# A decoder layer on one core: feed-forward weight pieces rounded and cast by ScalarE, limited by GpSimd, and the attention stage's side work put at other steps

## The chip, the cores and the metric

The kernel runs on one core of a Trainium2 chip. The metric is the device time of one execution in microseconds; each kernel is given with the median of its runs. The profile is of one execution of its own.

## The reference

One decoder layer over x (4 x 512 tokens x 512) and a context (4 x 512 x 256), in three stages that each end in a layer norm:

```python
x = _layernorm(x + _L0_attn_ref(x, q, k, v, o weights and biases))   # 32 heads of 16
x = _layernorm(x + _L0_xattn_ref(x, ctx_1024, Wq, bq, Wk, bk))
x = _layernorm(x + _L0_ffn_ref(x, w_gate, w_up, w_down))             # 512 -> 2048 -> 512
```

The attention quantizes its weights to 4 bits, and its activations in chunks of 64 tokens: per chunk the channel bias is taken away, each channel gets one of 8 scales by comparing its maximum with thresholds, and values are rounded to that scale. The same is done again to the attention's result before the output projection. The feed-forward weights are ternary:

```python
scale = jnp.clip(jnp.mean(jnp.abs(w)), EPS)
q = jnp.clip(jnp.round(w / scale), -1.0, 1.0) * scale
```

## The kernel before, in words

Everything is written out by hand for the five engines; each engine runs its own list in order and waits on semaphores. There are three stages: preparation (sums of weights, x decomposed), the attention stage, and the rest (output projection, cross attention, feed-forward). The change is in the attention stage.

**Groups and steps.** The attention stage goes through 32 groups (`NG`), numbered n = 0 to 31: batch b = n // 8, four heads r = n % 8. Each group has 8 steps, u = 0 to 7, and every engine has a function for one group: `pe_period`, `act_period`, `dve_period`, `pool_period`, `sp_period`. "Even" groups are those with n even. In the text a time "in the group" is counted from the group's transpose of the row maxima (`pe_nm`, L1134), which TensorE issues at the end of step 1. A group's length is the time from its transpose to the next one.

**TensorE** does in each step twice: a 128x512 score tile of the next group (`pe_scores`, L1129, three banks, so tile t waits until VectorE has read tile t - 3), and a transposed score tile of an earlier group (`pe_scores_T`, L1150, three banks, so tile t waits until ScalarE has taken the exponential of tile t - 3). At four steps, `PV_AT`, it multiplies a quarter of the probabilities by the values (`pe_pv`, L1164). In even groups it projects the next tile of queries and keys at steps 3 and 5 (`QK_AT`, `pe_qk`, L333 and L334), in odd groups the values at step 5 (`pe_v`, L1115 and L1117).

**VectorE** takes a maximum of each score tile (`dve_max`, L1277), splits the 16 maxima of a group in three bf16 terms at steps 0 and 1 (`dve_nm`, L1284 to L1293) for the transpose, scales queries and keys (`dve_y`, L353), and does the side work in `dve_context`, after the tiles of the step: for the attention's result of batch b - 2 the maximum (`dve_tmax`), eleven threshold steps (`dve_levels`), and the final values (`dve_n`, L1017).

**ScalarE** takes the exponentials (L1237, two per step), copies pieces out, and at step 3 of groups 0 to 23 rounds one piece of the feed-forward weights by adding a large constant (`act_ffn`, L1393, 128x1024 f32 in place). `act_round` (L1013) rounds the attention's result at r = 3.

**GpSimd** works the query and key parts (`pool_parts`), normalizes (`pool_norm`), and finishes a weight piece in two operations (`pool_ffn`): L1399 limits it to the constant plus or minus 1, L1401 takes the constant away and writes bf16 into `f_int_all`. Then it centers (`pool_center`, r = 7) or scales (`pool_scale`, r = 1) the attention's result.

**SyncE** issues the DMAs in one order: the transposed maxima, stacks of queries and keys, in odd groups the spread of the reciprocal sums and the attention's result (`sp_spread`, which for b >= 2 waits until all of `dve_n` of two batches before is done), stores, and the next weight piece (`sp_ffn`). The ring for weight pieces has two slots.

```python
PV_AT, QK_AT, V_AT, HIGH_AT, MIDDLE_AT = (1, 2, 6, 7), (3, 5), 5, (4, 6), (5, 7)
```

Of the kernel before, what the change touches and what calls it, by code (L numbers as in the profile page):

```python
# [18 lines left out]
P = 128  # L19
# [28 lines left out]
def decoder_layer(nc, io):  # L48
    whole = ExitStack()
    with whole:  # L50
# [19 lines left out]
        had = keep("had", [P, P])  # L70
        magic = keep("magic", [P, 1])
        chunk_of = keep("chunk_of", [96, NB, S], BF16)
        n_T = keep("n_T", [P, KD, NB, S], BF16)
# [329 lines left out]
        with stage:  # L403
# [194 lines left out]
            with nc.Block() as block:  # L598
# [135 lines left out]
                @block.gpsimd  # L734
                def _(pool):
                    pool.memset(onesf[:], 1.0)
                    pool.memset(sv_col[:], 1.0)
# [330 lines left out]
        with stage:  # L1068
# [37 lines left out]

            PV_AT, QK_AT, V_AT, HIGH_AT, MIDDLE_AT = (1, 2, 6, 7), (3, 5), 5, (4, 6), (5, 7)
            def v_bank(kt):
# [143 lines left out]
            def act_period(act, g):  # L1252
                even = g.h == 0
                for u in range(8):
# [5 lines left out]
                    if even and g.has(2):  # L1260
                        if u in HIGH_AT:
                            act_high(act, g.tile(2), HIGH_AT.index(u))
                        if u in MIDDLE_AT:
                            act_middle(act, g.tile(2), MIDDLE_AT.index(u))
                    if g.b > 1 and g.r == 3 and 1 <= u <= 4:
                        act_round(act, g.b - 2, u - 1)
                    if u == 3 and g.n < PIECES:
                        act_ffn(act, g.n)
                    if not even and u == V_AT + 1 and g.b < NB - 1:

                        if g.b and g.s == 0:
                            act.wait_ge(pv_mm, 2 * 2 * KD * g.b)
                        act_v(act, g.b + 1, g.s)
# [39 lines left out]
            def dve_context(dve, g, u):  # L1313
# [10 lines left out]
                if g.b > 1 and g.r == 0:  # L1324
                    if u == 0:
                        dve_tmax(dve, g.b - 2, misc)
                    else:
                        dve_levels(dve, g.b - 2, u - 1)
                if g.b > 1 and g.r == 1 and u < 4:
                    dve_levels(dve, g.b - 2, 7 + u)  # L1330
                if g.b > 1 and g.r == 3 and u > 4:
                    dve_n(dve, g.b - 2, u - 5)
                if g.b > 1 and g.r == 4 and u == 0:
                    dve_n(dve, g.b - 2, 3)
                if g.b == NB - 1:
# [8 lines left out]
            def pool_period(pool, g):  # L1344
                if g.h == 0 and g.has(2):
                    pool_parts(pool, g.tile(2))
                if g.h == 1 and g.n >= 5:
                    pool_norm(pool, (g.n - 5) // 2, rs_bc[:])
                if g.n < PIECES:
                    pool_ffn(pool, g.n)  # L1350
                if g.b and g.r == 7:
                    for ct in range(KD):
                        pool_center(pool, g.b - 1, ct)
                if g.b > 1 and g.r == 1:
                    for ct in range(KD):
                        pool_scale(pool, g.b - 2, ct)

            def sp_pv(sp, g):
# [4 lines left out]
            def sp_period(sp, g):  # L1363
# [16 lines left out]
                if g.n == PIECES:  # L1380
                    need(sp, "f_done", 2 * PIECES)
                    load_wo(sp, woT[:], bo_row[:])
# [4 lines left out]
            def sp_ffn(sp, c):  # L1387
                need(sp, "f_done", 2 * (c - 1))
                sp.dma_start(f_ring[:, c % 2, :], io["ffn"][c]).then_inc(f_in[c % 2], 16)
# [6 lines left out]
            def pool_ffn(pool, c):  # L1396
                raw = f_ring[:, c % 2, :]
                need(pool, "f_round", c + 1)
                did(pool.tensor_scalar(raw, raw, MAGIC - 1.0, MAGIC + 1.0, ALU.max, ALU.min), "f_done")  # L1399
                need(pool, "f_done", 2 * c + 1)  # L1400
                did(pool.tensor_scalar(f_int_all[:, c, :], raw, -MAGIC, None, ALU.add), "f_done")  # L1401

# [923 lines left out]
```

## Time and profile before

| what | before |
|---|---|
| median of 3 runs | 1176.83 us (1174.73 to 1180.32) |
| time of the profiled execution | 1178.66 us |
| its span | 1176.9 us |
| PE busy | 955.5 us (81%) |
| DVE busy | 863.0 us (73%) |
| ACT busy | 688.4 us (58%) |
| POOL busy | 388.9 us (33%) |

The busy shares are averages over three stages. The attention stage lies from about 142 us to 619 us of the span.

### The profile page before, as it was taken

To read this page: it belongs to the slowest core of one execution; us is meant where nothing else is said; L and a number is where in the kernel's file an instruction comes from. 1 tells how busy PE (TensorE), PEld (TensorE's weight loads), DVE (VectorE), ACT (ScalarE), POOL (GpSimd) and SP (SyncE) were. 2 spreads that over 40 slices of the span, in tenths; PEclk is the share of its full clock that TensorE was granted. 3 is DMA by queue.
4 is the path that set the end of the run, shared out by engine and by line. 5 is a ranking of instruction groups with operands and counts; after the bars stand their busy time and mean duration, and the time that the engine had idled before them with its cause. 6 is when DMAs were issued, how large, how long until landed. Compare 5 with 4: busy or idle time off the path is not lost. (4 is left out here: it accounts for less than half of the span.)

```text
span 1176.9 us, 13444 instructions
## 1 busy us (share of the span) xinstructions
PE 955.5 (81%) x4128; PEld 369.3 (31%) x4128; DVE 863.0 (73%) x1622; ACT 688.4 (58%) x1103; POOL 388.9 (33%) x303
## 2 busy tenths in 40 slices
PE   3667799889998888988887678797989798879465
PEld 1223322222222222222122343343434343434122
DVE  7996688888899989999883658568656765575245
ACT  3778377777777677767564034265526562555255
POOL 4103355656665676653002423130014001400000
PEclk9779699999999999999999879999999899989788
DMA  8966455555556554546334102310251025002500
GB/s 306 350 234 213 163 153 164 170 180 181 182 181 181 163 172 153 177 138 178 92 101 137 56 38 64 80 72 1 58 120 73 1 53 120 7 1 61 118 1 36
DMA packets 90684, 145.00 MB, mean 123 GB/s; under 512 B 12339, under 2 KB 52147, under 8 KB 89078
## 3 DMA queue, kind: packets, MB, share of 16 engines
q1 hardware_dynamic: 90614, 144.16, 40.7%
q8 instruction: 33, 0.54, 0.2%
q14 instruction: 37, 0.30, 0.1%
HBM read 84.75 MB, written 42.21 MB: 108 GB/s over the span
## 5 line engine op out<-in xcount | busy, mean ns | idle before, releaser
L1277 DVE TENSOR_REDUCE neg_max<-banks 128x1 f32<-128x512 f32 x512 | 331.4, 683 | 48.2 <-PE banks L1129 44.7
L1237 ACT ACTIVATE probs<-banks 128x512 f32<-128x512 f32 x512 | 278.3, 600 | 116.3 <-PE banks L1150 115.5
L1129 PE MATMUL banks<-k_st,q_st 96*128 96x512 bf16 x512 | 198.0, 392 | 20.9 <-DVE neg_max L1277 18.4
L1150 PE MATMUL banks<-q_st,k_st 99*128 99x512 bf16 x512 | 195.4, 385 | 13.2 <-ACT probs L1237 9.3
L1164 PE MATMUL banks<-probs,v_st 128*32 128x512 f32 x1024 | 137.1, 607 | 17.5 <-ACT pv_z L1250 16.3
L1543 POOL TENSOR_TENSOR rstd<-vare,half 128x1 f32<-128x1 f32 x48 | 26.8, 558 | 358.7 <-DVE vare L1535 358.7
L1749 PE MATMUL banks<-q_T,f_int_all 128*128 128x512 bf16 x512 | 127.5, 391 | 19.5 <-DVE h_ring L1770 19.4
L1129 PEld LDWEIGHTS banks<-k_st,q_st 96*128 96x128 bf16 x512 | 50.4, 99 | 171.2 <-DVE neg_max L1277 105.3
L1808 PE MATMUL banks<-hz,I_h 128*128 128x512 f32 x128 | 67.9, 667 | 34.5 <-DMA hz<-h_turned 32.1
L1759 DVE TENSOR_TENSOR h_ring<-banks,gate_row 128x512 f32<-128x512 f32 x64 | 44.1, 689 | 60.3 <-PE banks L1749 58.5
L1399 POOL TENSOR_SCALAR woT<-woT 128x1024 f32<-128x1024 f32 x24 | 87.2, 3633 | 2.4 <-ACT woT L1393 0.4
L1764 ACT ACTIVATE h_ring<-h_ring 128x512 f32<-128x512 f32 x64 | 40.3, 630 | 79.5 <-DVE h_ring L1759 79.5
L1749 PEld LDWEIGHTS banks<-q_T,f_int_all 128*128 128x128 bf16 x512 | 49.0, 100 | 101.2 <-DVE h_ring L1770 28.8
L1787 ACT COPY h_turned<-banks 128x512 f32<-128x512 f32 x64 | 37.1, 582 | 61.1 <-DMA hz<-h_turned 36.3
L1150 PEld LDWEIGHTS banks<-q_st,k_st 99*128 99x128 bf16 x512 | 49.9, 98 | 64.7 <-ACT probs L1237 22.1
L1891 PE MATMUL banks<-f_int_all,ctx_q 128*128 128x512 bf16 x256 | 61.1, 386 | 9.1 <-ACT ctx_q L1875 9.1
L1527 PE MATMUL banks<-attn_T,x_T 128*128 128x512 f32 x128 | 60.8, 619 | 9.1 <-DVE x L1566 7.5
L906 POOL TENSOR_TENSOR ctx_q<-ctx_q,rs_bc 128x512 f32<-128x512 f32 x14 | 17.8, 1269 | 151.7 <-DMA ctx_q<-pv_rows 151.7
L1827 DVE TENSOR_TENSOR h_max<-h_abs,h_max 128x512 f32<-128x512 f32 x60 | 45.0, 751 | 30.7 <-ACT h_abs L1816 29.4
L1401 POOL TENSOR_SCALAR f_int_all<-woT 128x1024 bf16<-128x1024 f32 x24 | 66.7, 2778 | 2.0
L1813 ACT COPY hz<-banks 128x1024 f32<-128x1024 f32 x32 | 32.4, 1014 | 58.8 <-PE banks L1808 58.7
L1781 PE MATMUL banks<-h_ring,had 128*128 128x512 f32 x128 | 64.4, 596 | 2.1 <-ACT h_turned L1787 2.1
(263 smaller groups left out, 1519.1 us busy)
## 6 DMA issues: line engine op xcount, KB each, us to landing
hz<-h_turned SPq DMA_DIRECT2D x64, 256.0 KB
f_int_all<-in_ffn_dram SPq DMA_DIRECT2D x24, 512.0 KB, 8.6
qk_parts<-parts SPq DMA_DIRECT2D x32, 384.0 KB, 2.5
q_st<-qk_parts SPq DMA_DIRECT2D x32, 384.0 KB, 3.9
k_st<-qk_parts SPq DMA_DIRECT2D x32, 384.0 KB, 4.9
woT<-in_ffn_dram SPq DMA_DIRECT2D x24, 512.0 KB, 3.4
qk_parts<-parts SPq DMA_DIRECT2D x32, 256.0 KB, 2.9
pv_rows<-pv_z SPq DMA_DIRECT2D x32, 256.0 KB, 5.1
```

Source lines behind the costliest of these rows:

```text
L1129: pe.matmul(s_bank[(16 * g.n + tile) % SB], q_st[g.i][0:KR, j, qt * P:(qt + 1) * P], k_st[g.i][0:KR, j, :], start=True, stop=True).then_in ...
L1150: pe.matmul(st_bank[at % STB], k_st[g.i][:, j, kt * P:(kt + 1) * P], q_st[g.i][:, j, :], start=True, stop=True).then_inc(st_mm, 1)
L1164: last = pe.matmul(pv_bank[32 * j:32 * j + 32, :], v_st[g.v][:, kt].rearrange("p h d -> p (h d)")[:, (HD + 1) * head:(HD + 1) * head + 2 * ...
L1237: act.activation(probs[ktp][:, j, i, :], st_bank[(16 * g.n + 2 * w + i) % STB], ACT.Exp).then_inc(exp_done, 2)
L1277: dve.tensor_reduce(neg_max[:, g.h, tile:tile + 1], s_bank[(16 * g.n + tile) % SB], AX.X, ALU.max, negate=True).then_inc(max_done, 1)
L1399: did(pool.tensor_scalar(raw, raw, MAGIC - 1.0, MAGIC + 1.0, ALU.max, ALU.min), "f_done")
L1401: did(pool.tensor_scalar(f_int_all[:, c, :], raw, -MAGIC, None, ALU.add), "f_done")
L1527: last = pe.matmul(bank, x1_T[:, k, t], attn_T[:, k, :], start=k == 0, stop=k == KD - 1)
L1749: last = pe.matmul(bank, f_int[w][:, k * FF + ch.start:k * FF + ch.stop], q1_T[:, k, :], start=k == 0, stop=k == KD - 1)
L1781: did(pe.matmul(H_BANK[i % 2], had[:], h[:, g % HRING, :], start=True, stop=True), "h1_mm")
L1808: last = pe.matmul(pair_banks(p)[:, a, :], I8_h16[:], hz[:, 2 * p + a, :], start=True, stop=True)
L1891: last = pe.matmul(down_bank(b, t), q2_T[:, k, token_tile(t)], f_int["down"][:, k * D:(k + 1) * D], start=k == 0, stop=k == FK - 1)
```

## The change

ScalarE now does two operations on a weight piece and GpSimd one: round (ScalarE, as before), limit (GpSimd, as before but now last in its group), and a second ScalarE operation, `act_ffn_store`, one group later at step 3, which takes the constant away and writes bf16. The SyncE waits count ScalarE's store. The value product at step 1 moves to steps 2 and 3. The threshold steps move from steps 1 to 7 of r = 0 and 0 to 3 of r = 1 to the odd steps of r = 0 and steps 1 to 7 of r = 1. The scaling moves from r = 1 to r = 2, behind the parts. The roundings move from steps 1 to 4 to steps 1, 3, 5, 7, and the final values from (3,5) (3,6) (3,7) (4,0) to (3,7) (4,0) (5,1) (5,6), as (r, step).

```diff
+            N_AT = ((3, 7), (4, 0), (5, 1), (5, 6))
-            PV_AT, QK_AT, V_AT, HIGH_AT, MIDDLE_AT = (1, 2, 6, 7), (3, 5), 5, (4, 6), (5, 7)
+            PV_AT, QK_AT, V_AT, HIGH_AT, MIDDLE_AT = (2, 3, 6, 7), (3, 5), 5, (4, 6), (5, 7)
...
-                    if g.b > 1 and g.r == 3 and 1 <= u <= 4:
-                        act_round(act, g.b - 2, u - 1)
+                    if g.b > 1 and g.r == 3 and u % 2:
+                        act_round(act, g.b - 2, u // 2)
                     if u == 3 and g.n < PIECES:
                         act_ffn(act, g.n)
+                    if u == 3 and 0 < g.n <= PIECES:
+                        act_ffn_store(act, g.n - 1)
...
-                    else:
-                        dve_levels(dve, g.b - 2, u - 1)
-                if g.b > 1 and g.r == 1 and u < 4:
-                    dve_levels(dve, g.b - 2, 7 + u)
-                if g.b > 1 and g.r == 3 and u > 4:
-                    dve_n(dve, g.b - 2, u - 5)
-                if g.b > 1 and g.r == 4 and u == 0:
-                    dve_n(dve, g.b - 2, 3)
+                    if u % 2:
+                        dve_levels(dve, g.b - 2, u // 2)
+                if g.b > 1 and g.r == 1 and u:
+                    dve_levels(dve, g.b - 2, 3 + u)
+                if g.b > 1 and (g.r, u) in N_AT:
+                    dve_n(dve, g.b - 2, N_AT.index((g.r, u)))
...
-                if g.n < PIECES:
-                    pool_ffn(pool, g.n)
...
-                if g.b > 1 and g.r == 1:
+                if g.b > 1 and g.r == 2:
                     for ct in range(KD):
                         pool_scale(pool, g.b - 2, ct)
+                if g.n < PIECES:
+                    pool_ffn(pool, g.n)
...
             def sp_ffn(sp, c):
-                need(sp, "f_done", 2 * (c - 1))
+                need(sp, "f_done", c - 1)
...
-                did(pool.tensor_scalar(raw, raw, MAGIC - 1.0, MAGIC + 1.0, ALU.max, ALU.min), "f_done")
-                need(pool, "f_done", 2 * c + 1)
-                did(pool.tensor_scalar(f_int_all[:, c, :], raw, -MAGIC, None, ALU.add), "f_done")
+                did(pool.tensor_scalar(raw, raw, MAGIC - 1.0, MAGIC + 1.0, ALU.max, ALU.min), "f_clip")
+
+            def act_ffn_store(act, c):
+                need(act, "f_clip", c + 1)
+                did(act.activation(f_int_all[:, c, :], f_ring[:, c % 2, :], ACT.Identity, bias=neg_magic[:]), "f_done")
```

Three places in the order of instructions. First ScalarE in an odd group (from the copy of step 0 on; the value copy `v_st` belongs to step 6). Before:

```order
92 L1250 ACTIVATE pv_z<-banks,sv_col 128x512
93 L1237 ACTIVATE probs<-banks 128x512 x6
94 L1393 ACTIVATE woT<-woT,magic,f_rec 128x1024
95 L1237 ACTIVATE probs<-banks 128x512 x6
96 L1242 ACTIVATE v_st<-banks,tb_tok 128x32x16
```

After the change:

```order
94 L1253 ACTIVATE pv_z<-banks,sv_col 128x512
95 L1240 ACTIVATE probs<-banks 128x512 x6
96 L1396 ACTIVATE woT<-woT,magic,f_rec 128x1024
97 L1406 ACTIVATE f_int_all<-woT,neg_magic 128x1024
98 L1240 ACTIVATE probs<-banks 128x512 x6
99 L1245 ACTIVATE v_st<-banks,tb_tok 128x32x16
```

The second 128x1024 operation stands directly behind the first, ahead of the exponentials of step 4.

Second TensorE in even group 12, from the end of step 1 (`identb,nm` is the transpose) to the query projection of step 3 (L333). Before:

```order
515 L1164 MATMUL banks<-probs,v_st 32x512 x4
516 L1134 MATMUL banks<-identb,nm 128x128
517 L1129 MATMUL banks<-k_st,q_st 128x512
518 L1150 MATMUL banks<-q_st,k_st 128x512
519 L1129 MATMUL banks<-k_st,q_st 128x512
520 L1150 MATMUL banks<-q_st,k_st 128x512
521 L1164 MATMUL banks<-probs,v_st 32x512 x4
522 L1129 MATMUL banks<-k_st,q_st 128x512
523 L1150 MATMUL banks<-q_st,k_st 128x512
524 L1129 MATMUL banks<-k_st,q_st 128x512
525 L1150 MATMUL banks<-q_st,k_st 128x512
526 L333 MATMUL banks<-n_T,qk_x 128x512 x4
```

After the change:

```order
515 L1137 MATMUL banks<-identb,nm 128x128
516 L1132 MATMUL banks<-k_st,q_st 128x512
517 L1153 MATMUL banks<-q_st,k_st 128x512
518 L1132 MATMUL banks<-k_st,q_st 128x512
519 L1153 MATMUL banks<-q_st,k_st 128x512
520 L1167 MATMUL banks<-probs,v_st 32x512 x4
521 L1132 MATMUL banks<-k_st,q_st 128x512
522 L1153 MATMUL banks<-q_st,k_st 128x512
523 L1132 MATMUL banks<-k_st,q_st 128x512
524 L1153 MATMUL banks<-q_st,k_st 128x512
525 L1167 MATMUL banks<-probs,v_st 32x512 x4
526 L334 MATMUL banks<-n_T,qk_x 128x512 x4
```

One product left its place ahead of the transpose, and one now stands between the scores of step 3 and the query projection.

Third VectorE in group 16 (b = 2, r = 0), from the key scaling (`y<-banks,s_col_k`) of step 5 to the first term of the maxima. Before:

```order
379 L353 SCALAR_TENSOR_TENSOR y<-banks,s_col_k,tb_all 128x512
380 L978 TENSOR_TENSOR c_level<-c_level,c_tmax 128x7x8 x4
381 L1277 TENSOR_REDUCE neg_max<-banks 128x1 x2
382 L982 TENSOR_TENSOR c_level<-c_level,levels 128x224
383 L1277 TENSOR_REDUCE neg_max<-banks 128x1 x2
384 L984 TENSOR_REDUCE c_frac<-c_level 128x32
385 L1284 CAST nm<-neg_max 128x16
```

After the change:

```order
375 L354 SCALAR_TENSOR_TENSOR y<-banks,s_col_k,tb_all 128x512
376 L971 RECIPROCAL c_rtb<-c_tb 128x8
377 L973 COPY tbo_tok<-c_tb 64x4
378 L974 COPY tbo_tok<-c_tb 64x4
379 L1282 TENSOR_REDUCE neg_max<-banks 128x1 x4
380 L976 TENSOR_TENSOR c_level<-c_cmax,levels 128x224
381 L1289 CAST nm<-neg_max 128x16
```

The comparison with the thresholds (four operations), its product, the sum, and the step behind it left group 16 for group 17.

## Rows read from the trace of the kernel before

**Rows 1.** The transpose that begins each group, all 32: ns min/median/max, first and last start.

```profile
L1134 PE MATMUL banks<-identb,nm x32: 216/216/266, 142.4 to 618.6; 128*128 128x128 bf16 x32
```

**Rows 2.** Windows, groups 5, 12, 16, 18, 19, 21: us, busy by engine, PEclk, DMA.

```profile
215.80:231.40 15.60, 12.97 (x71) 3.95 (x72) 11.93 (x22) 10.75 (x19) 8.84 (x4) 1.00 0.66 195
321.30:336.34 15.04, 13.90 (x75) 4.42 (x76) 13.58 (x25) 12.09 (x22) 11.04 (x7) 1.00 0.55 175
...
381.26:400.19 18.93, 14.34 (x75) 4.15 (x76) 18.61 (x38) 12.33 (x22) 16.07 (x11) 1.00 0.47 153
...
414.92:431.45 16.53, 14.16 (x75) 4.39 (x75) 14.31 (x25) 12.18 (x23) 14.51 (x11) 1.00 0.47 146
431.45:449.93 18.48, 15.00 (x74) 4.16 (x71) 15.35 (x28) 13.13 (x23) 11.14 (x5) 0.91 0.59 175
...
464.98:479.25 14.27, 13.11 (x70) 3.90 (x70) 12.68 (x24) 10.63 (x19) 7.95 (x4) 1.00 0.66 201
```

**Rows 3.** Groups of instructions of the attention stage, the exponentials: busy, mean ns, idle before.

```profile
L1237 ACT ACTIVATE probs<-banks 128x512 f32<-128x512 f32 x490 | 266.8, 600 | 113.2 <-PE banks L1150 112.4 <-issue 0.2
```

**Rows 4.** Timeline of PE in odd group 13 (336.34 to 350.62): start us, us.

```profile
341.45 0.39 PE L1129 MATMUL banks<-k_st,q_st 96*128 96x512 bf16 x1 [0.55 <-DVE neg_max L1277]
341.84 0.39 PE L1150 MATMUL banks<-q_st,k_st 99*128 99x512 bf16 x1
...
350.62 0.23 PE L1134 MATMUL banks<-identb,nm 128*128 128x128 bf16 x1
```

**Rows 5.** Timeline of ACT in the same group: start us, us.

```profile
340.06 1.24 ACT L1393 ACTIVATE woT<-woT,magic,f_rec 128x1024 f32<-128x1024 f32 x1
341.19 2.06 ACT L1237 ACTIVATE probs<-banks 128x512 f32<-128x512 f32 x4
```

**Rows 6.** Timeline of ACT in odd group 5 (215.8 to 231.4).

```profile
220.81 1.24 ACT L1393 ACTIVATE woT<-woT,magic,f_rec 128x1024 f32<-128x1024 f32 x1 [1.17 <-DMA woT<-in_ffn_dram]
```

**Rows 7.** Timeline of PE in group 5.

```profile
222.59 0.39 PE L1150 MATMUL banks<-q_st,k_st 99*128 99x512 bf16 x1 [2.00 <-ACT probs L1237]
```

**Rows 8.** Timeline of PE in even group 12 (321.30 to 336.34).

```profile
324.20 1.03 PE L333 MATMUL banks<-n_T,qk_x 128*128 128x512 bf16 x4
...
334.89 1.07 PE L1164 MATMUL banks<-probs,v_st 128*32 128x512 f32 x8 [0.61 <-ACT pv_z L1250]
336.34 0.22 PE L1134 MATMUL banks<-identb,nm 128*128 128x128 bf16 x1 [0.39 <-DVE nm L1293]
```

**Rows 9.** Timeline of DVE: two rows of group 12, one of group 13.

```profile
325.48 0.75 DVE L353 SCALAR_TENSOR_TENSOR y<-banks,s_col_q,tb_all 128x512 f32<-128x512 f32 x1 [0.45 <-PE banks L334]
...
329.40 2.70 DVE L1277 TENSOR_REDUCE neg_max<-banks 128x1 f32<-128x512 f32 x4
...
350.24 0.16 DVE L1293 TENSOR_TENSOR nm<-nm_f,nm 128x16 bf16<-128x16 f32 x1
```

**Rows 10.** Single lines: ns min/median/max of one, first and last start.

```profile
L1393 ACT ACTIVATE woT<-woT,magic,f_rec x24: 1227/1240/1241, 140.1 to 498.5; 128x1024 f32<-128x1024 f32 x24
...
L1401 POOL TENSOR_SCALAR f_int_all<-woT x24: 2777/2778/2782, 159.6 to 511.5; 128x1024 bf16<-128x1024 f32 x24
...
L1287 DVE TENSOR_TENSOR nm_f<-neg_max,nm x32: 159/533/1145, 140.7 to 615.3; 128x16 f32<-128x16 f32 x32
```

**Rows 11.** The page's groups, a plain 128x1024 copy on ACT.

```profile
L1813 ACT COPY hz<-banks 128x1024 f32<-128x1024 f32 x32 | 32.4, 1014 | 58.8 <-PE banks L1808 58.7
```

**Rows 12.** Timeline of DVE in group 16, and the final values' group by form.

```profile
392.03 1.46 DVE L978 TENSOR_TENSOR c_level<-c_level,c_tmax 128x56 f32<-128x56 f32 x4
...
L1017 DVE SCALAR_TENSOR_TENSOR n_T<-ctx_q,c_frac 128x512 bf16<-128x512 f32 x16 | 12.1, 757 | 0.2
```

**Rows 13.** Timeline of SP in group 21: the spread and the next weight piece.

```profile
468.77 0.66 SPq L894 DMA_DIRECT2D rs_bc<-rs_rows  x1
...
476.93 0.46 SPq L1389 DMA_DIRECT2D woT<-in_ffn_dram  x1
```

**Rows 14.** The page's DMA issues: KB, median us to landing.

```profile
woT<-in_ffn_dram SPq DMA_DIRECT2D x24, 512.0 KB, 3.4
```

More of the change, by code:

```diff
@@ L71, in decoder_layer @@
         magic = keep("magic", [P, 1])
+        neg_magic = keep("neg_magic", [P, 1])
         chunk_of = keep("chunk_of", [96, NB, S], BF16)
@@ L735, in _ @@
                 def _(pool):
+                    pool.memset(neg_magic[:], -MAGIC)
                     pool.memset(onesf[:], 1.0)
@@ L1380, in sp_period @@
                 if g.n == PIECES:
-                    need(sp, "f_done", 2 * PIECES)
+                    need(sp, "f_done", PIECES)
                     load_wo(sp, woT[:], bo_row[:])
```

## The prediction

> **What bounds the kernel now.** I read first the transposes that begin the groups, to get the rhythm: 32 of them over 476 us [rows 1], so all that the change touches is in 476 of 1177 us, about 15 us a group. Then the windows of single groups [rows 2]. An ordinary even group (12) takes 15.04 us with PE busy 13.90 and DVE 13.58; an ordinary odd one (21) takes 14.27 with 13.11 and 12.68. ACT is busy 12.1 and 10.6. So PE and DVE bound a group together, and ACT has room on average: its exponentials waited 113 us for PE over the stage [rows 3]. The exceptions are groups 16 (18.93 us, DVE busy 18.61: the threshold steps), 18 (16.53: GpSimd busy 14.51, its scaling ahead of the parts) and 19 (18.48: roundings and final values). They recur as 24 and 27. Those stalls are what the moves of side work can win.
>
> Then the timelines, because room on average says nothing of one step. In odd group 13, ACT rounds the weight piece at 340.06 and can begin the exponentials of step 4 only at 341.19 [rows 5]; the first is done 0.6 us later, at about 341.8, and at 341.84 PE issues the transposed tile that waited for that bank [rows 4]. ACT's weight operation is on the path in every odd group. Group 5 shows the price: there the piece landed late, ACT ran L1393 at 220.81, which is 5.01 in the group instead of 3.72 [rows 6], PE waited 2.00 us [rows 7], and the group took 15.60 instead of 14.27 [rows 2]. A delay of ACT of 1.3 us at that place cost 1.3 us. From there to the end of the group PE runs without a pause, so nothing gives it back.
>
> **ACT's second operation.** The store is 128x1024 f32 to bf16 with a bias pointer. Bounds: 1.01 us, a plain copy of that size [rows 11], and 1.24, the rounding with bias and scale pointers [rows 10]. Consecutive ACT operations overlap by 0.1 (1.24 long, next one 1.13 later [rows 5]), so it adds 0.9 to 1.14. I take 1.14, nearest in form. The Trainium skill (ScalarE: Activation LUTs, What ACT_TABLE_LOAD costs) gives an ACTIVATE with one bias pointer 280 ns plus 0.833 ns per element, an estimate of 1.13 us for the store; by that the term would be 1.04 a group, about 1 us less in all.
> In odd groups the whole of it is paid, as in group 5. The product moved to step 3 adds nothing there: PE waited 0.55 us for DVE before 341.45 [rows 4], and the tile behind now waits for ACT anyway. Ten ordinary odd groups (1 to 15, 21, 23): 10 x 1.14 = **+11.4**. The GpSimd limit, now later, ends before ACT's step 3 in ordinary groups, since GpSimd's cast of 2.78 us [rows 10] is gone.
>
> **The product at step 3.** One product holds PE 1.0 us (334.89 to about 335.9 [rows 8]). In even groups it now stands ahead of the query projection, which today follows the scores directly at 324.20 [rows 8], and whose result DVE awaited 0.45 us at 325.48 [rows 9]. From there DVE has no pause until the last maximum: four of them run 2.70 us in one piece at 329.40 [rows 9]. So the group gets 1.09 us longer in its body. What does step 1 give back? In group 12 the transpose was released not by the product but by DVE's third term (0.39 us wait at 336.34 [rows 8]): nothing. In odd group 13 it starts as the product ends, at 350.62 [rows 4], but DVE's term is ready only at 350.40 [rows 9]: at most 0.1. ACT's store in even groups ends at about 6.1 in the group, its first exponential of step 4 at 6.6, before PE, itself 1.09 later, wants that bank at about 6.9: hidden by the product, as the product would be by it in part. Ten ordinary even groups (2 to 14, 20, 22, 26): 10 x 1.09 = **+10.9**. Group 0 has neither.
>
> **Threshold steps.** Four leave group 16 for 17, and 24 for 25: 1.46 us [rows 12] and three of some 0.4, together 2.6. Group 16 loses 2.6, gains 1.1 by the product, and its second step leaves step 2, where it stood in a short DVE wait, for step 3, where DVE is full (an estimate of 0.6, the size of the waits in [rows 4, 9]): -0.9, the same in 24. Group 17 has DVE at its limit with 2.6 more, of which 0.4 falls in a wait: +2.2, the same in 25. Sum **+2.6**. The steps are spread, but DVE has no free time to spread them into.
>
> **Scaling, roundings, final values.** Group 18 loses its 1.5 us of excess over an ordinary even group and gains 1.1: -0.4. Group 19 gives two final values of 0.7 us [rows 12] to group 21 (-1.4), and about half of what the clock cost there (0.91 granted [rows 2], 1.7 us of 18.48), and pays the store: -1.0. Group 27 gives two values and pays the product beside the bias work: 0. Group 21 takes two values, mostly in waits: +0.2. Sum **-1.2**.
>
> **A new wait on SyncE.** The spread of group 21 is issued 3.8 in the group (468.77 against 464.98) and the next weight piece 8.2 behind it [rows 13], [rows 2]. The spread waits for the last final value, now at step 6, about 10.9 in. The stores behind it and the piece for group 22 move with it: issued about 19.1, landed 3.4 later [rows 14], at 22.5, where group 21 ends at about 15.5. ACT wants the piece at 3.7 in group 22 and gets it at 7.0: of the 3.3, 0.3 to 0.5 is hidden by the product, so **+2.5** (between 0 and 3.3). The same wait in group 29 has no piece behind it.
>
> **The last groups.** 28 and 30 pay part of the product, 29 little: **+1.6**.
>
> **Sum:** 11.4 + 10.9 + 2.6 - 1.2 + 2.5 + 1.6 = 27.8 us on the profiled 1178.66, so about 1206.5; the median lies 1.8 lower, so **1204.6 us**. The other stages don't change.
>
> **The rivals.** *A, the room is enough (faster).* ACT's 113 us of waits [rows 3] take the store, the product at step 3 lies in the hole of that step in even groups as well, and only the stalls shrink: 1.5 in 18, two final values and the clock in 19 and 27 (3 each), 2.6 less 1.0 in 16 and 24: about 11 us, so 1166. It decides where the first exponential of step 4 comes more than 1.1 us before PE wants its bank. Against it: group 5. Chance 0.06.
> *B, one of the two costs hides (slower by less).* If even groups pay nothing because PE had waited there anyway, the 10.9 go: 1194. For it: PE has 1.1 us idle in an even group [rows 2]; against: that idle lies at the transpose. Chance 0.17.
> *C, the clock falls (slower by more).* Even groups now have PE idle for 2.2 us before each transpose. In group 19 two waits close together went before a fall to 1.2 GHz (0.91 mean [rows 2]) that cost some 1.7 us; in group 5 one wait of 2.00 us didn't (1.00). If ten of the groups pay 1.3 each: 1218. Chance 0.15.
> *D, DVE is relieved by GpSimd (slower by less, or near the same).* DVE's small term L1287 takes between 159 and 1145 ns, median 533 [rows 10], longest while GpSimd works. If the 24 casts gone bring it to 159, 0.37 us in 23 groups, 8.6 us return; with L1290 and the threshold steps at the same, some 20: 1185 to 1196. That GpSimd and VectorE share SBUF interfaces is a rule of the Trainium skill (Advanced Engine Details and Errata, GPSIMD Details), which speaks for this rival. Against it: the casts ran from about 1.8 to 4.6 in a group, the terms at 12 to 15, beside the parts and the limit, which stay. Chance 0.10.
> No change at all would need A's savings and half of the costs together: 0.05. My forecast keeps 0.47.
>
> **How the numbers follow.** A measurement of this kernel can tell about 0.5%, 5.9 us, from no change. Faster: A, 0.07. Same: the tail of D and mixtures, 0.06. Slower: the rest, 0.87. The range goes from D and B's lower side, 1187, to C, 1221; below it lie A and the mixtures, above it a stronger C.
>
> **What would show it.** Right: odd groups at 15.4 and even ones at 16.1 us; in odd groups PE's wait for ACT's exponential ahead of the second transposed tile of step 5; in even groups a wait of 2 us for DVE's L1298 ahead of the transpose, and none for `pv_z`; group 17 near 17 us, group 22 above 18. Wrong: ordinary groups unchanged with the store in place (A), even groups near 15 (B), PEclk under 0.95 in the stage (C), L1292 near 0.16 us (D), or a store far from 1.2 us.

## The result and the profile after

| | before | after |
|---|---|---|
| median of 4 runs each, on one chip | 1178.57 us | 1207.24 us (1197.8 to 1211.11) |
| ratio, with its 95% interval | 1 | 1.0258 [1.0194, 1.0323] |
| span of the profiled execution | 1176.9 us | 1207.2 us |
| from the first to the last group transpose | 476.2 us | 508.5 us |

The change makes the kernel 2.6% slower (between 1.9 and 3.2%), and all of it lies in the attention stage: 32.3 us more there, 2 us less outside. Of all executions in this document one was slow, one of the ten of run 6 with 2364.54 us, and it isn't in that run's ratio (the median given there is of all ten). Two groups from the page after the change, the exponentials and the products:

```profile
L1240 ACT ACTIVATE probs<-banks 128x512 f32<-128x512 f32 x512 | 278.7, 599 | 126.1 <-PE banks L1153 124.6
L1167 PE MATMUL banks<-probs,v_st 128*32 128x512 f32 x1024 | 146.7, 647 | 1.0 <-ACT probs L1240 1.0
```

The products no longer wait for the copy `pv_z` (0.6 us a group before [rows 8]). ACT has one more operation a group and yet waits for PE longer than before: 126.1 us, where the page before has 116.3 (for the stage alone 123.2, against the 113.2 of [rows 3]). Windows of groups 5, 12, 13, 16, 18, 19, 21, 22 and 30, which answer to [rows 2]; columns are us, busy of PE, PEld, DVE, ACT, POOL, granted clock, DMA:

```profile
218.70:234.10 15.40, 12.77 (x69) 3.79 (x71) 10.64 (x22) 11.11 (x19) 5.82 (x3) 1.00 0.67 197
329.80:345.90 16.10, 13.79 (x75) 4.34 (x77) 13.48 (x25) 13.24 (x23) 7.60 (x6) 1.00 0.48 146
345.90:361.60 15.70, 14.35 (x70) 3.97 (x72) 12.40 (x24) 11.13 (x19) 6.25 (x3) 0.89 0.64 192
394.20:413.20 19.00, 15.72 (x75) 4.35 (x77) 15.64 (x31) 13.47 (x23) 11.80 (x7) 0.91 0.43 134
428.70:446.60 17.90, 15.36 (x75) 4.46 (x77) 13.74 (x25) 13.96 (x24) 7.90 (x8) 0.90 0.43 133
446.60:464.00 17.40, 14.39 (x69) 3.92 (x71) 13.29 (x26) 13.61 (x23) 10.33 (x5) 0.91 0.57 170
480.10:496.20 16.10, 14.41 (x70) 3.98 (x72) 13.00 (x26) 11.15 (x19) 1.74 (x1) 0.89 0.47 136
496.20:514.90 18.70, 14.05 (x75) 4.21 (x77) 14.34 (x31) 13.79 (x25) 10.75 (x7) 1.00 0.51 154
633.60:651.20 17.60, 13.15 (x61) 3.29 (x62) 9.97 (x25) 7.92 (x15) 1.28 (x1) 0.81 0.30 99
```

Group 12 is 1.0 us longer, with PE and DVE busy for as long as before within 0.12 us: that is every undisturbed even group. Groups 13, 16, 18, 19 and 21 have a granted clock of about 0.9; before, of the groups shown, only 19 had. Counted by the trace's clock, it falls to 1.2 GHz twelve times in the stage, where it fell three times before, and the granted clock over the stage is 0.94 instead of 0.98. Group 30 is 4.5 us longer than its 13.13.

Three places explain an ordinary group. First PE and ACT in odd group 3 (188.1 to 202.6), which answer to [rows 4] and [rows 5]:

```profile
194.65 0.39 PE L1153 MATMUL banks<-q_st,k_st 99*128 99x512 bf16 x1 [0.85 <-ACT probs L1240]
...
202.60 0.22 PE L1137 MATMUL banks<-identb,nm 128*128 128x128 bf16 x1 [0.79 <-DVE nm L1298]
```

```profile
192.96 1.14 ACT L1406 ACTIVATE f_int_all<-woT,neg_magic 128x1024 bf16<-128x1024 f32 x1
194.00 2.06 ACT L1240 ACTIVATE probs<-banks 128x512 f32<-128x512 f32 x4
```

The store runs, the exponential of step 4 begins 1.04 us later than it would, and PE's second transposed tile of step 5 waits for it: 6.53 in the group instead of 5.50. The first half is as forecast. But the group is only 0.2 us longer than before, 14.48. The end shows why, in DVE's rows of the same group:

```profile
200.93 0.17 DVE L1292 TENSOR_TENSOR nm_f<-neg_max,nm 128x16 f32<-128x16 f32 x1
201.01 0.68 DVE L1282 TENSOR_REDUCE neg_max<-banks 128x1 f32<-128x512 f32 x1
201.61 0.16 DVE L1295 CAST nm<-nm_f 128x16 bf16<-128x16 f32 x1
201.68 0.68 DVE L1282 TENSOR_REDUCE neg_max<-banks 128x1 f32<-128x512 f32 x1
202.28 0.17 DVE L1298 TENSOR_TENSOR nm<-nm_f,nm 128x16 bf16<-128x16 f32 x1
```

With the terms at 0.17 us each the transpose comes 2.7 us after the first score tile of step 0. Before, with the product and its wait for `pv_z` ahead of it, it was 3.54 us. That returns 0.84. Both parts are needed for it: run 1 below, with the product gone but slower terms, gives back 0.3, and run 2, with fast terms but the product there, nothing. In group 13 before the change two of the terms were slower:

```profile
348.12 0.49 DVE L1287 TENSOR_TENSOR nm_f<-neg_max,nm 128x16 f32<-128x16 f32 x1
...
349.13 0.60 DVE L1290 CAST nm<-nm_f 128x16 bf16<-128x16 f32 x1
```

Where a GpSimd operation lies beside the terms they are slower after the change too, and less comes back (group 11: 3.46 us).

Second, the end of even group 12, answering to the last of [rows 8]:

```profile
345.87 0.22 PE L1137 MATMUL banks<-identb,nm 128*128 128x128 bf16 x1 [2.01 <-DVE nm L1298]
```

PE now has nothing to do for 2 us. Third, what can follow such a hole, PE at the start of group 7:

```profile
250.19 0.22 PE L1137 MATMUL banks<-identb,nm 128*128 128x128 bf16 x1 [2.01 <-DVE nm L1298]
...
250.47 0.38 PE L1153 MATMUL banks<-q_st,k_st 99*128 99x512 bf16 x1
250.69 0.38 PE L1132 MATMUL banks<-k_st,q_st 96*128 96x512 bf16 x1
...
251.21 1.44 PE L1167 MATMUL banks<-probs,v_st 128*32 128x512 f32 x8
...
252.99 0.63 PE L1153 MATMUL banks<-q_st,k_st 99*128 99x512 bf16 x1
253.41 0.63 PE L1132 MATMUL banks<-k_st,q_st 96*128 96x512 bf16 x1
```

Matmuls stand first 0.22 us apart and then 0.42: the engine runs at 1.2 GHz. Group 7 takes 15.97 us. (It took 15.48 before, without a fall, so the clock isn't the only thing that makes it long.)

At last the two long groups. SyncE in group 29 and PE in group 30, then ACT and PE in group 22:

```profile
630.07 0.66 SPq L896 DMA_DIRECT2D rs_bc<-rs_rows  x1
...
637.04 0.46 SPq L1388 DMA_DIRECT2D qk_x<-in_x_dram  x1
637.54 0.90 SPq L1368 DMA_DIRECT2D q_st<-nm_T  x1
```

```profile
642.93 0.61 PE L1153 MATMUL banks<-q_st,k_st 99*128 99x512 bf16 x1 [4.11 <-DMA q_st<-nm_T]
```

```profile
503.21 1.24 ACT L1396 ACTIVATE woT<-woT,magic,f_rec 128x1024 f32<-128x1024 f32 x1 [3.21 <-DMA woT<-in_ffn_dram]
```

```profile
503.74 0.39 PE L1153 MATMUL banks<-q_st,k_st 99*128 99x512 bf16 x1 [1.23 <-DMA q_st<-nm_T]
506.02 0.39 PE L1153 MATMUL banks<-q_st,k_st 99*128 99x512 bf16 x1 [1.68 <-ACT probs L1240]
```

The spread waits for the last final value, and everything behind it on SyncE comes late. In group 22 ACT gets its weight piece 7.0 us in the group, which is what the prediction said. In group 30 the small transfer of the maxima is issued 0.5 us behind a 1 MB load of x, and PE gets it 5.4 us after its issue. Before, it was issued 3.7 us behind that load, and PE went on with it 2.3 us later.

### The profile page after: what moved, and what is told of

It reads as the page before. It is cut to its first block, busy times and chain, and to the rows that moved or that the text cites. A ratio compares the mean times of both kernels' runs of the same rounds, so it can differ in the third digit from the quotient of the medians.

```text
span 1207.2 us, 13391 instructions
## 1 busy us (share of the span) xinstructions
PE 962.0 (80%) x4076; PEld 368.7 (31%) x4128; DVE 853.9 (71%) x1622; ACT 714.9 (59%) x1127; POOL 323.6 (27%) x280
## 4 chain that ended last, share of the span: by engine, by line
PE 46%; DVE 23%; issue 8%; DMA 5%; ACT 3%; POOL 3%; SPq 0%; POOLq 0%; DVEq 0%; ACTq 0%
DVE neg_max L1282 10%; PE banks L1167 9%; PE banks L1132 6%; PE banks L1754 6%; PE banks L1153 6%; PE banks L1896 4%; PE banks L1786 3%; DMA hz<-h_turned 3%; PE banks L1532 3%; PE banks L1813 2%; PE banks L334 2%; POOL y L1641 2%; DVE h_max L1832 1%; DVE h_ring L1775 1%; DMA pv_rows<-pv_z 1%
## 5 line engine op out<-in xcount | busy, mean ns | idle before, releaser
L1240 ACT ACTIVATE probs<-banks 128x512 f32<-128x512 f32 x512 | 278.7, 599 | 126.1 <-PE banks L1153 124.6
L1153 PE MATMUL banks<-q_st,k_st 99*128 99x512 bf16 x512 | 200.7, 395 | 21.4 <-ACT probs L1240 15.0
L1132 PE MATMUL banks<-k_st,q_st 96*128 96x512 bf16 x512 | 202.3, 400 | 12.9 <-DVE neg_max L1282 10.4
L1167 PE MATMUL banks<-probs,v_st 128*32 128x512 f32 x1024 | 146.7, 647 | 1.0 <-ACT probs L1240 1.0
L1754 PE MATMUL banks<-q_T,f_int_all 128*128 128x512 bf16 x498 | 124.2, 388 | 21.5 <-DVE h_ring L1775 19.7
L365 POOL TENSOR_TENSOR rest<-y,parts 128x512 f32<-128x512 f32 x32 | 37.1, 1160 | 130.8 <-ACT parts L343 130.7
```

The lines of the kernel that those rows point to most:

```text
L1132: pe.matmul(s_bank[(16 * g.n + tile) % SB], q_st[g.i][0:KR, j, qt * P:(qt + 1) * P], k_st[g.i][0:KR, j, :], start=True, stop=True).then_in ...
L1153: pe.matmul(st_bank[at % STB], k_st[g.i][:, j, kt * P:(kt + 1) * P], q_st[g.i][:, j, :], start=True, stop=True).then_inc(st_mm, 1)
L1167: last = pe.matmul(pv_bank[32 * j:32 * j + 32, :], v_st[g.v][:, kt].rearrange("p h d -> p (h d)")[:, (HD + 1) * head:(HD + 1) * head + 2 * ...
L1240: act.activation(probs[ktp][:, j, i, :], st_bank[(16 * g.n + 2 * w + i) % STB], ACT.Exp).then_inc(exp_done, 2)
L1754: last = pe.matmul(bank, f_int[w][:, k * FF + ch.start:k * FF + ch.stop], q1_T[:, k, :], start=k == 0, stop=k == KD - 1)
```

## The experiments

Group lengths below are differences between transposes; "clean" groups are ordinary ones in which the clock didn't fall. Group lengths and falls come from the one profiled execution of each kernel. Twelve kernels ran. Ratios are to the kernel before, which was timed beside them each time (medians of 1175.95, 1177.33 and 1177.48 us).

**1. The products alone.**

```diff
-            PV_AT, QK_AT, V_AT, HIGH_AT, MIDDLE_AT = (1, 2, 6, 7), (3, 5), 5, (4, 6), (5, 7)
+            PV_AT, QK_AT, V_AT, HIGH_AT, MIDDLE_AT = (2, 3, 6, 7), (3, 5), 5, (4, 6), (5, 7)
```

> Before, with the value products alone at steps 2, 3, 6, 7 instead of 1, 2, 6, 7. Theory (the product holds PE ahead of the query projection, and the transpose waits for DVE anyway): ordinary even groups 16.1 us instead of 15.04; odd groups the same or some tenths shorter, because their PE waited for DVE at step 5 and the product no longer stands ahead of the transpose; in all about +12 us, 1190, plus 1 to 2 us for each fall of the clock in the stage. Rival (step 3 has a hole for it in even groups too): even groups stay near 15.0 and the time within 3 us of before.

Measured 1197.28 us, ratio 1.0178 [1.0152, 1.0205]. Even groups 15.99, odd ones 13.95 (group 1) to 14.12 (group 11), and eleven falls of the clock. One stands at this transpose, and the matmuls behind it take 0.63 us:

```profile
184.78 0.26 PE L1134 MATMUL banks<-identb,nm 128*128 128x128 bf16 x1 [1.92 <-DVE nm L1293]
```

The product costs an even group 0.94 and gives an odd one 0.3 back. Over 15 pairs that is about 10 us; the rest of the 18.5 us that the stage grew stands in groups in or beside which the clock fell (3: 16.50, 20: 19.02, 25: 17.23, where without a fall about 14, 16 and 14.6 stand).

**2. The store alone**, at step 3 of the next group, GpSimd's cast gone, all else as before (the lines of `act_ffn_store`, `pool_ffn` and `sp_ffn` in the change's diff).

> Before, with ScalarE's second operation on each weight piece at step 3 and GpSimd's cast gone, nothing else moved. Theory (the first exponential of step 4 is on PE's path): odd groups about 15.3 us instead of 14.27, even groups about 15.8 (there PE wants the bank at 5.8 in the group and gets it at 6.6), so 23 groups at 0.8 to 1.1, about +20 us, 1199. Rival A (ACT has room on average): no group gets longer and the time is within 3 us of before. Rival D (GpSimd's cast disturbed DVE's small operations): DVE's L1287 sinks from a median of 533 ns toward 160 and the groups end 0.4 us sooner.

Measured 1199.37 us, 1.0196 [1.0165, 1.0227]. Clean odd groups 15.32, even ones 15.59. ACT, and PE in group 3 (190.2 to 205.5):

```profile
195.05 1.14 ACT L1407 ACTIVATE f_int_all<-woT,neg_magic 128x1024 bf16<-128x1024 f32 x1
196.09 1.07 ACT L1239 ACTIVATE probs<-banks 128x512 f32<-128x512 f32 x2
```

```profile
196.73 0.39 PE L1152 MATMUL banks<-q_st,k_st 99*128 99x512 bf16 x1 [1.71 <-ACT probs L1239]
...
204.51 1.06 PE L1166 MATMUL banks<-probs,v_st 128*32 128x512 f32 x8 [0.61 <-ACT pv_z L1252]
205.50 0.23 PE L1136 MATMUL banks<-identb,nm 128*128 128x128 bf16 x1
```

Rival A falls: with the products in their old place the odd group pays the store in full, 1.05 us. The clock falls nine times, here at the wait of step 5 (groups 1, 5, 7, 11: 16.9 to 20.1 us). Rival D holds in part: without the casts groups 16, 18 and 24 sink by 1.8, 0.95 and 2.1 us, and L1287's counterpart has a median of 165 ns, not 533; but that is not the casts' doing, as run 8 shows (see the last section).

**3. The changed kernel with the products back** (the line of run 1, reversed).

> The changed kernel with the value products back at steps 1, 2, 6, 7. If the store at step 3 alone already costs an even group some 0.8 us, the product at step 3 lies mostly in its shadow: then even groups sink only from 16.08 to about 15.8, odd groups rise from 14.5 to 15.3 where the product stands ahead of the transpose again, and the time is within 8 us of the changed kernel's 1207. If the two costs add up in even groups instead, they sink to about 15.0 and the time to about 1195.

Measured 1204.99 us, 1.0242 [1.022, 1.0264]. Even 15.59, odd 15.32, as in run 2: the first case. With the store at step 3, moving the product costs an even group 0.49 and gives an odd one 0.84 back. So beside this store the moved product costs nothing on balance, and the two kernels are the same within the intervals.

**4. The changed kernel, final values earlier.**

```diff
-            N_AT = ((3, 7), (4, 0), (5, 1), (5, 6))
+            N_AT = ((3, 7), (4, 0), (4, 4), (5, 1))
```

> The changed kernel with the last two final values at (4,4) and (5,1) instead of (5,1) and (5,6), so that SyncE's spread in groups 21 and 29 finds them done. Theory (the late values hold SyncE's queue, and with it the weight piece for group 22 and the maxima of group 30, which then land behind the 1 MB load of x): group 22 from 18.72 to about 16.6 and group 30 from 17.6 to about 13.5, together 5 to 7 us less than the changed kernel, about 1201. Rival (the two long groups come from DVE or from the clock): no more than 1.5 us gained.

Measured 1196.47 us, 1.0183 [1.0147, 1.022]. SyncE in group 21:

```profile
486.45 0.66 SPq L896 DMA_DIRECT2D rs_bc<-rs_rows  x1
...
495.17 0.46 SPq L1392 DMA_DIRECT2D woT<-in_ffn_dram  x1
```

Nothing holds the spread, group 22 takes 16.53 instead of 18.72 and group 30 13.34 instead of 17.63: 6.5 us as expected. The time sank by more than the 5 to 7 us expected: 0.8% by the ratios, whose intervals overlap. The profiled stage is 13.9 us shorter; what goes beyond the two groups stands mostly in groups 7, 13, 21, 24, 26 and 27, where the clock fell in the changed kernel and not here. It fell nine times instead of twelve. Why there were fewer falls isn't shown.

**5. The changed kernel without the store** (GpSimd limits and casts at its new place).

> The changed kernel with GpSimd doing the limit and the cast again, behind its other work, and no second operation on ScalarE. Theory: odd groups 14.0 to 14.1 as with the products moved alone, even groups 16.0, DVE's small operations slower again, group 22 and 30 still long by SyncE's wait; the store's share is what is missing against 1207: about 6 to 10 us, so 1198 to 1201. If the store is what costs most, as my first sum had it for odd groups (1.14 each), it sinks by 15 or more.

Measured 1201.83 us, 1.0192 [1.0162, 1.0222]. Even 15.98, odd 13.54 to 14.13, sixteen falls. Beside the products the store costs 5 us by the medians and 8 by the ratios, not the 11.4 that I had for the odd groups alone. The intervals of the two kernels overlap and the clock falls more often here, so the size isn't firm.

**6. The moves of side work alone** (store and products both undone).

> The changed kernel with both undone, the store and the products: only the threshold steps, the scaling, roundings, final values and GpSimd's order are as in the change. Theory: ordinary groups as before (15.05 and 14.27), 18 and 19 shorter by 1 to 1.5 each, 16 shorter and 17 longer by 2, group 22 longer by 1.5 to 3 and 30 by 4 through SyncE's wait; within 5 us of before, 1173 to 1181. Rival (the side work as moved carries a good part of the loss): more than 8 us above before.

Measured 1179.12 us, 1.0017 [0.9991, 1.0044]. The time is as expected. Ordinary groups as before; 16 and 17 together 32.18 instead of 33.66, 18 and 19 31.3 instead of 35.0; but 22 takes 17.33 and 30 20.64. Gain and loss cancel.

**7. The same, with the final values of run 4.**

> The moves of side work alone (store and products undone), with the last final values at (4,4) and (5,1). Against the moves alone, group 22 should sink from 17.33 to 15.5 and group 30 from 20.64 to 13.1, so 7 to 9 us: 1169 to 1173. What it shows is whether the moves of threshold steps, scaling and roundings gain anything by themselves once SyncE isn't held: by the groups 2 to 5 us less than before. Rival: SyncE's wait is not what made 30 long, and the time stays at 1177 to 1180.

Measured 1168.79 us, 0.9936 [0.9907, 0.9965]. Group 22 is 15.52, group 30 13.15. The moves by themselves gain some 0.6%, once nothing holds SyncE.

**8. The store at step 2 of the next group**, nothing else changed against run 2:

```diff
-                    if u == 3 and 0 < g.n <= PIECES:
+                    if u == 2 and 0 < g.n <= PIECES:
```

> Before with ScalarE's store, but at step 2 of the next group, where ACT waits 0.9 us for PE in each group, and GpSimd's limit ends at 1.8 in it. Theory (what costs is the place and not the operation): the exponentials of step 3 begin at most 0.3 us late, ordinary groups grow by 0 to 0.3 us instead of 0.5 (even) and 1.05 (odd), and groups 16, 18 and 24 keep the 1 to 2 us each that they win without GpSimd's cast; the time is 1170 to 1180, against 1199 with the store at step 3. Rival (ACT or the missing room costs it anyway): above 1188.

Measured 1170.73 us, 0.9933 [0.9905, 0.9961]. ACT in an odd group:

```profile
337.93 1.08 ACT L1239 ACTIVATE probs<-banks 128x512 f32<-128x512 f32 x2 [1.44 <-PE banks L1152]
338.93 1.15 ACT L1407 ACTIVATE f_int_all<-woT,neg_magic 128x1024 bf16<-128x1024 f32 x1
339.98 1.06 ACT L1239 ACTIVATE probs<-banks 128x512 f32<-128x512 f32 x2
```

Before, the exponentials of step 3 in group 13 had this wait ahead of them:

```profile
339.09 1.08 ACT L1237 ACTIVATE probs<-banks 128x512 f32<-128x512 f32 x2 [0.89 <-PE banks L1150]
```

The store now lies in those 0.89 us; the odd group is 14.33, the even one 15.09. One step earlier the same operation costs 0.05 us instead of 1.05 in an odd group, and the whole kernel is 29 us faster than in run 2. That settles that its place costs, not its work. How much of the 29 us is the clock, which falls twice here and nine times there, isn't separated.

**9. The hole ahead of the transpose filled.**

```diff
+                        if g.h == 1:
+                            for _ in range(4):
+                                pe.matmul(misc, identb[0:96, :], chunk_of[:, 0, :], start=True, stop=True)
                         pe_nm(pe, g)
```

> The changed kernel with four matmuls more ahead of the transpose of odd groups, in the 2.2 us for which TensorE sits there idle after an even group; they write a bank that the transpose overwrites, so nothing else changes. Theory (the clock falls, twelve in the stage against three before, come from that hole, since seven of the first ones lie within 2 us behind such a transpose): the hole shrinks to 1.3 us, even groups stay at 16.1 because DVE releases the transpose, the falls sink to three or four and the time by 8 to 15 us, to about 1195. Rival (the falls come from the new wait for ACT at step 5, or from PE's lower share in general): the number of falls stays at eight or more and the time within 4 us of 1207.

Measured 1206.14 us, 1.023 [1.0205, 1.0256]. PE at the end of group 6, and the windows of the stage's two parts (this run, then the changed kernel):

```profile
249.11 1.03 PE L1209 MATMUL banks<-chunk_of,identb 96*128 96x512 bf16 x4
251.18 0.23 PE L1137 MATMUL banks<-identb,nm 128*128 128x128 bf16 x1 [1.04 <-DVE nm L1301]
```

```profile
142.60:368.00 225.40, 200.63 (x1050) 61.41 (x1050) 184.45 (x341) 176.11 (x304) 90.38 (x48) 0.98 0.55 166
368.00:644.00 276.00, 237.46 (x1198) 67.46 (x1196) 227.54 (x452) 190.97 (x335) 94.17 (x62) 0.95 0.47 141
```

```profile
142.70:378.00 235.30, 203.39 (x1038) 60.95 (x1052) 190.36 (x352) 182.42 (x315) 95.98 (x52) 0.96 0.54 162
378.00:651.20 273.20, 229.06 (x1123) 63.52 (x1135) 220.55 (x437) 185.17 (x325) 88.76 (x58) 0.93 0.46 138
```

(The two profiles' windows end at other groups, so only the clock is to be compared.) The falls sink from twelve to six, with none left before group 16, and the stage from 508.5 to 501.9 us in the profiles. The four other kernels with these holes (runs 1, 4, 5, 12) had three to five falls before group 16, as the changed kernel has three, so there the hole is the likely cause. The time didn't follow: 8 to 15 us were expected, and the ratios' intervals overlap. Over the four executions of each kernel the granted clock rose only from 0.923 to 0.927 on average (the kernel before has about 0.935). Groups 22 and 30, held by SyncE, came out longer in this profile (20.2 and 20.1), with one fall in each. The clock's share in the time isn't settled by this run.

**10. Run 8 with roundings at steps 1, 3, 5, 7 and final values at (3,7) (4,0) (4,4) (5,1).**

```diff
+            N_AT = ((3, 7), (4, 0), (4, 4), (5, 1))
...
-                    if g.b > 1 and g.r == 3 and 1 <= u <= 4:
-                        act_round(act, g.b - 2, u - 1)
+                    if g.b > 1 and g.r == 3 and u % 2:
+                        act_round(act, g.b - 2, u // 2)
```

> Before with the store at step 2 of the next group (as in the run that gained 0.7%), the roundings at steps 1, 3, 5, 7 and the final values at (3,7) (4,0) (4,4) (5,1); threshold steps, scaling and products as before. Group 19 should sink from 16.8 to about 16.1 and 27 from 18.9 to about 17, with no new wait of SyncE: 2 to 3 us under the store at step 2 alone, so a ratio to before of about 0.991. Rival (the values only move their cost to groups 20 and 21): the same as the store at step 2 alone, 0.993.

Measured 1167.57 us, 0.9918 [0.9891, 0.9945]: the fastest version. Group 27 is 16.83 instead of 18.92 in run 8, 19 is 16.98 instead of 16.80. Against run 8 alone the gain is within the intervals.

**11. The changed kernel with three things put right**: store at step 2, old products, final values as in run 4.

> The changed kernel with three things put right: the store at step 2, the products back at 1, 2, 6, 7, and the last final values at (4,4) and (5,1). If store at step 3, products and SyncE's wait are the whole loss, ordinary groups are 15.1 and 14.4 again, 22 and 30 are 15.6 and 13.2, and the time is 30 to 36 us under the changed kernel's 1207: 1169 to 1176. If something else of the change costs, it stays above 1180.

Measured 1178.76 us, 1.0015 [0.9986, 1.0044], just outside what I expected. Ordinary groups are 15.09 and 14.33, 22 and 30 are 15.58 and 13.13, but 16 takes 22.13 and 19 21.17. ACT in group 16:

```profile
388.22 1.15 ACT L1406 ACTIVATE f_int_all<-woT,neg_magic 128x1024 bf16<-128x1024 f32 x1 [4.71 <-POOL woT L1402]
```

GpSimd's limit stands behind the centering and the scaling there, as the change put it, and ends too late for step 2. In run 8, where the limit is ahead of them, these groups take 17.22 and 16.80. So the order "limit last" and the earlier store don't go together. That the order alone makes up the rest of this run's loss is argued from these two groups; no run has the limit ahead with everything else as here.

**12. The changed kernel, store alone at step 2.**

> The changed kernel with the store alone at step 2 instead of 3. Theory (in even groups the product at step 3 is a cost of its own, as large as the store's and hiding it): even groups stay at 16.0, odd ones sink by no more than 0.5 because their end is set by DVE's terms; the falls of the clock stay; 1197 to 1204. Rival (the store at step 3 was the reason for both): even groups sink to 15.1 too and the time to 1185 or less.

Measured 1211.87 us, 1.0299 [1.0252, 1.0345]; its profiled execution took 1206.6. Even groups 15.98: the rival falls. The odd group 3 sank by 0.97, more than I expected, and yet nothing came of it: fifteen falls of the clock, and 22.56 us in group 22. There the store waited 5.58 us for GpSimd's limit, which stood behind a normalization that the late spread of group 21 held; the round behind the store then didn't wait for its piece. The expected time was missed by 8 us on the slow side.

The clean groups side by side (even / odd, us; even groups of 2 to 12, odd group 3; in the first row of the last column groups 1, 9 and 11 of runs 1 and 5, because in group 3 of these runs the clock was down):

| | product as before | product at steps 2 and 3 |
|---|---|---|
| no store | 15.05 / 14.27 | 15.99 / 13.5 to 14.1 |
| store at step 3 | 15.59 / 15.32 | 16.08 / 14.48 |
| store at step 2 | 15.09 / 14.33 | 15.98 / 13.51 |

## Why the prediction was right or wrong

The total was near (1204.6 for 1207.24) and the direction and the places were right: the store, the product at step 3 and the wait on SyncE each cost what runs 1, 2 and 4 show. But that the total is so near is partly luck. The store's term was too large, the clock's was nothing, and the two errors cancel. Two of the signs that the prediction named for being wrong came as well (the clock of the stage under 0.95, L1292 near 0.16 us), and one for being right didn't (group 17 near 17 us). By its own steps, with group lengths of the two profiles:

- **ACT's second operation: the delay right, its sum too large.** The store takes 1.14 us, and the next operation begins 1.04 behind its start (I added 1.14 a group). The formula of the Trainium skill (ScalarE: Activation LUTs, What ACT_TABLE_LOAD costs) gave 1.13 for the whole; by it the term was 1.04, and the trace agrees with both. The store delays PE by 1.03 in odd groups. But the nine odd groups 1 to 15 and 23 grew by 7.1 us and not 10.3, and that with three falls of the clock among them (with group 21, which had a fall too, 8.9 for 11.4); the undisturbed group 3 grew by 0.2. The sentence that failed is "at most 0.1" for what the vacated step 1 gives back in odd groups: I read DVE's term of group 13, where GpSimd's work slowed it, as the floor. Without it DVE is ready 0.8 us earlier (group 3 after the change). In runs 2 and 3, where the product stands there, the odd groups pay the 1.05 forecast.
- **The product at step 3: right.** The seven even groups 2 to 14 grew by 1.0 each (forecast 1.09). That it hides the store there is shown by runs 2, 3 and 5: an even group has 15.98 without the store, 16.08 with it, and 15.59 with the store alone. Group 26, counted among the ordinary ones, grew by 3.2: 0.5 through the moved side work (15.11 in run 6), 1.1 through the product (16.20 in run 4), and 1.6 in this profile, where the clock fell in it.
- **Threshold steps: the sum near, one half wrong.** Groups 16, 17, 24 and 25 grew by 1.8 (forecast 2.6), although the clock fell in 16 and 24. Run 6 shows what the moves do without store and product: 16 sank by 2.1, as the prediction has it, but 17 grew by 0.6 and not by 2.2, so the two are 1.5 us shorter. The step that fails is "DVE has no free time to spread them into": in group 17 it had most of what was needed, and after the change that group takes 15.57 us.
- **Scaling, roundings, values: -1.2 forecast.** 18, 19 and 27 grew by 2.5. 19 sank by 1.05 as forecast. 18 and 27 had falls of the clock; without one, 18 takes 16.20 in runs 5 and 12, 0.3 less than before, as forecast, and 27 takes 17.68 in run 9.
- **The wait on SyncE: the mechanism right, half of it missed.** Group 22 grew by 3.2 for 1.1 + 2.5. For group 29 I wrote that it "has no piece behind it": it has the 1 MB load and the maxima of the next group. Group 30 grew by 4.5; the last groups were to pay 1.6 together. Run 4 takes both back.
- **Rival C came in part.** Twelve falls for three. How much of the 32.3 us is theirs is open. An estimate: groups 7, 9, 13, 21, 24 and 27 are together 8.9 us longer than in run 9, group 18 is 1.7 longer than in run 12 and 26 1.6 longer than in run 4, where the clock didn't fall in them. That makes 12 us. The three falls before the change have to be taken off, at the 1.7 us that the prediction read for one of them, so some 7 us are left. Against it stands that run 9, which removed half of the falls, took 6.6 us from the stage in the profile and nothing that the runs could tell.
- **A falls** by run 2: with nothing else moved, ACT's waits didn't take the store at step 3. Run 8 shows that they do one step earlier, which the prediction didn't ask. **B falls** by runs 1 and 12: the product costs an even group 0.94 without a store and 0.89 beside one at step 2, which by itself costs it 0.03. **D** came as a sign and not as a cause: the median of the small term sank to 170 ns, but run 8, without the casts, keeps 535 (last section). What the missing casts do give is about 5 us in groups 16, 18 and 24 (runs 2 and 8), which the prediction had left out.

## What to carry to other kernels

Free time of an engine counts at the step where the work is put: giving GpSimd's cast to ScalarE cost 23 us in the whole kernel at one step and gained 8 at the step before, where the engine had been waiting (both by the ratios of runs 2 and 8). Before giving an engine more, look in its timeline for the wait that will take it, and check that its input is ready by then. When work is put off, look at what waits for it in an in-order DMA queue and at what is queued behind that.

## What the runs showed of the hardware that I hadn't expected

DVE's 128x16 subtraction takes 159 to 176 ns when GpSimd is idle, and up to 1.1 us beside GpSimd's two-input operations. Beside its limit, which has one input, it took 0.16 us in some groups and 0.6 in others. Its row after the change, answering to the last of [rows 10], and the store's:

```profile
L1292 DVE TENSOR_TENSOR nm_f<-neg_max,nm x32: 159/170/959, 141.1 to 649.8; 128x16 f32<-128x16 f32 x32
```

```profile
L1406 ACT ACTIVATE f_int_all<-woT,neg_magic x24: 1131/1142/1149, 162.4 to 536.6; 128x1024 bf16<-128x1024 f32 x24
```

The median is 170 ns and was 533. With GpSimd's cast gone and the groups as long as before the median stayed at 535 (run 8), so it wasn't the cast; with the cast kept and the side work moved it is 452 and 318 (runs 5 and 6). In the timelines it lay beside GpSimd's normalization (a two-input operation) in nine groups before and in none after; the groups end later, which is the likely reason. The parts' second operation still lies beside it in even groups.

A single 2 us wait of PE was followed by a fall of the clock to 1.2 GHz in some groups and not in others, in the changed kernel as in runs 1, 5 and 12; in the kernel before, the 2.00 us of group 5 passed without a fall. What decides between them no run shows.
